# Audio tower on one core: MOE0's weights split in the first stage, logits by groups of four tiles, MOE1's rows scattered into the result

## The chip, the cores and the metric

The kernel runs on one core of a Trainium2 chip. The metric is the device time of one launch in microseconds (us). All work and all data movement of the launch is in it: inputs and the result lie in the device's DRAM.

## The reference

x is (4, 64, 750), taken as 4 batches of 750 tokens; the result is (4, 750, 192), 3000 tokens of E = 192. In f32:

```
h = token mixer(x)                       # three attention blocks over pooled rows, kernels of 3, 5, 7
h = h + linear_attention(layernorm(h))   # 12 heads, features [1, x/rrd, x*x/rd]
h = h + moe0(layernorm(h))               # rms norm, softmax of 8 logits, top 2,
                                         # silu(gate) * up, width 384, down, times the probability;
                                         # plus its own input
h = h + window_attention(layernorm(h))   # 12 heads of 64, relative positions
h = h + moe1(layernorm(h))               # softmax of 8 logits, top 1, gelu, width 768, biases,
                                         # times the largest probability
```

## The kernel before, in words

h is held in SBUF as 24 tiles of P = 125 tokens. Four stages follow each other, and between two of them `Stage.close` (L118 to L124) clears the semaphores on POOL, so nothing of one stage overlaps the next: `token_mixer_and_attention` (0 to 116 us), `moe` with MOE0 (121 to 413), `window_attention` (422 to 1588), `moe` with MOE1 (1592 to the end). Each engine has its own instruction list, written by hand in its block of the stage, and waits on semaphores; the order in a block is the order in which the engine works. SP issues the DMAs, POOL the indirect ones.

`moe` serves both expert stages. `w1` holds for each of eight experts four quarters: the first 128 rows rounded (quarter 0) and their remainder (1), and the last 64 rows rounded (2) and the remainder (3, of which the lower half is zeroed by POOL, L915). ACT rounds (`round_weights`, L1093 to L1095), DVE subtracts (`rest_of_weights`, L1181 and L1182), since products run as fp32r with the parts added up. The front of the stage: DVE makes statistics (L1149, L1153) and the reciprocals and squares around L1163, then normalises tile by tile (`n`, L1171; in MOE0 `xn` = n times the rms factor and the row of norm weights, L1175). PE transposes a tile in two halves of 96 columns (L986), ACT copies them (`xnT`, L1104), and PE multiplies (L977): the tile `xnT` is the stationary operand and the 8 columns of `wr` move. SP stores `xn` to X in DRAM (L850 to L854, eight DMAs). DVE copies the logits (L1198; MOE1 adds the bias row, L1200), ACT takes the exponential (L1109), DVE the softmax (L1204 to L1206), the best one or two experts (L1210 to L1219) and the mask (L1223 or L1225). PE ranks the tokens of each expert (L997, L998), and DVE derives positions (L1229 to L1250) and the expert of each slot tile (`eid`, L1237 to L1241). A slot tile is 128 tokens of one expert: 54 in MOE0, 31 in MOE1.

Token numbers are put into slots by products: `tile0` says which slot tile a token goes to (L1258), `lane1` which lane in it (L1263, one operation for each of `top`), `tile1` is tile0 times the token's number, in two parts: the tile number by POOL (L922), the row number by DVE (L1268). 48 products in MOE0, 24 in MOE1 (L1005), give `who`, from which DVE works out the row to write (`give`, L1280) and to read (`take`, L1286).

Then come the slot tiles, in a ring of four buffers (13 turns and 2 tiles in MOE0, 7 and 3 in MOE1). POOL gathers 128 rows of X into `xg` (L928) after copying their numbers (L939, L949); PE transposes them (L1012, L1013), ACT and DVE split them (L1112 to L1115, L1294 and L1295, `rest_of_tokens`), PE makes the first products (L1023), ACT applies Silu or Gelu (L1127, L1131), DVE multiplies (L1303), PE transposes the hidden rows (L1059), DVE copies (L1309), PE makes the second products (L1073), DVE copies `y` or adds the bias (L1321, L1325), and POOL scatters it to Y in DRAM (L933).

After MOE0, SP loads Y back into the room of the next stage; h += n was added on DVE ahead of the logits' copy (L1189). After MOE1, SP loads Y (L873, eight DMAs), DVE adds each tile times its probability to h (L1347, 24 operations), and SP stores h to the result (L882, eight DMAs).

In stage 1, ACT and DVE also round and split the attention's weights (`w4`, from `raw`), which SP stores as W4 for the third stage. In `window_attention`, a head has six chunks, and SP moves its row of maxima, transposed by PE, as a row of the stationary operand (`max_row`, L1614, six DMAs for a head on semaphore `s_md`); PE waits for them before the head's scores (L1971).

## Time and profile before

| | us |
|---|---|
| median of 3 runs | 1837.29 (1833.49 to 1843.19) |
| the profiled execution | 1845.31 |
| its span | 1843.6 |
| PE busy | 1575.8 (85%) |
| DVE busy | 1190.7 (65%) |
| ACT busy | 1000.7 (54%) |
| POOL busy | 350.5 (19%) |
| TensorE clock granted, mean | 0.895 |

The span runs from the first to the last instruction that the profiler saw; the launch adds 1.7 to it. Busy shares are means over stages of different kinds: the attention takes 63% of the span and keeps PE near full, while the low places among the page's forty slices, at 7 to 12%, 22% and 86 to 90% of the span and in its last slice, are fronts and ends of stages.

### The profile page before, as it was taken

The page shows a single profiled execution, that of the slowest core. Times are in us where ns is not written, and L with a number is a line of the kernel's source. Part 1 is how long each engine was busy: PE and PEld are TensorE (multiplying, and loading weights), DVE is VectorE, ACT ScalarE, POOL GpSimd, SP SyncE. Part 2 cuts the span into 40 slices and gives each one's busy share as a digit, 9 for nine tenths or more (in the row PEclk, how much of TensorE's full clock was granted, in tenths as well). Part 3 has the DMA queues.
Part 4 walks back from the last instruction along what each step waited for, and adds up shares of the span by engine and source line. Part 5 has one row for each costly group of instructions (what it writes and reads, how often), then busy time and mean ns, then how long its engine had stood idle before and what let it go on. Part 6 is the DMA issues. An engine that isn't in the chain of part 4 may idle for free. (4 is left out here: it accounts for less than half of the span.)

```text
span 1843.6 us, 32271 instructions
## 1 busy us (share of the span) xinstructions
PE 1575.8 (85%) x10779; PEld 1476.3 (80%) x10780; DVE 1190.7 (65%) x2207; ACT 1000.7 (54%) x1781; POOL 350.5 (19%) x495
## 2 busy tenths in 40 slices
PE   5864599983699999899899899899999899648993
PEld 4764588873599899899899899899899898538993
DVE  3588555546686786786687686687786686562333
ACT  4134133323578577678578678578578577233330
POOL 4040366652010010010010010010010010213441
PEclk6875699996899899999899999899999899658997
DMA  5034011118010010110010110010010100441114
GB/s 192 16 80 136 22 55 52 55 50 209 17 50 10 27 51 10 29 50 10 27 50 10 29 48 12 28 42 18 28 42 18 28 8 18 128 166 34 43 42 116
DMA packets 66847, 94.72 MB, mean 51 GB/s; under 512 B 17824, under 2 KB 52338, under 8 KB 66330
## 3 DMA queue, kind: packets, MB, share of 16 engines
q1 hardware_dynamic: 58026, 75.19, 14.0%
q0 software_dynamic: 8688, 17.80, 3.4%
q8 instruction: 78, 1.28, 0.3%
q14 instruction: 55, 0.45, 0.1%
HBM read 71.71 MB, written 21.06 MB: 50 GB/s over the span
## 5 line engine op out<-in xcount | busy, mean ns | idle before, releaser
L2471 DVE TENSOR_TENSOR a_Plo<-a_PT,a_Phi 125x756 fp32r<-125x756 f32 x288 | 281.8, 979 | 72.5 <-ACT a_PT L2196 71.4
L2196 ACT ACTIVATE a_Phi<-a_S 125x756 fp32r<-125x756 f32 x288 | 231.2, 803 | 156.8 <-PE a_O L1990 128.8
L2361 DVE TENSOR_REDUCE a_nmx<-a_M 125x1 f32<-125x752 f32 x248 | 232.7, 938 | 108.2 <-PE a_M L1865 107.1
L1685 POOL TENSOR_TENSOR a_qlo<-a_work,a_qhi 127x750 fp32r<-127x750 f32 x48 | 79.2, 1656 | 1019.3 <-PE a_S L1971 514.9
L2196 ACT ACTIVATE a_PT<-a_S 125x756 f32<-125x756 f32 x288 | 230.2, 799 | 0.0
L1023 PE MATMUL m_psG<-m_w,m_xT 128*128 x788 | 169.7, 355 | 5.4 <-DVE m_xT L1295 4.2
L1971 PE MATMUL a_S<-a_qhi,a_khi 128*125 128x378 f32 x576 | 154.0, 349 | 13.8 <-DMA a_qhi<-a_mrow 7.5
L1983 PE MATMUL a_O<-a_Phi,a_vhi 125*128 125x378 f32 x576 | 150.2, 342 | 1.4 <-issue 1.1
L1023 PEld LDWEIGHTS m_psG<-m_w,m_xT 128*128 128x128 f32 x788 | 138.7, 194 | 12.9 <-issue 11.5
L1971 PE MATMUL a_S<-a_qhi,a_klo 128*125 128x378 f32 x576 | 148.5, 339 | 0.0
L1971 PE MATMUL a_S<-a_qlo,a_khi 128*125 128x378 f32 x576 | 147.9, 338 | 0.0
L1990 PE MATMUL a_O<-a_Plo,a_vhi 125*128 125x378 f32 x576 | 147.6, 337 | 0.4 <-DVE a_Plo L2471 0.2
L1986 PE MATMUL a_O<-a_Phi,a_vlo 125*64 125x378 f32 x576 | 146.6, 336 | 0.0
L1073 PE MATMUL m_psY<-m_w,m_hidT 128*128 x696 | 128.0, 328 | 1.9 <-DVE m_hidT L1309 1.9
L1865 PE MATMUL a_M<-a_khi,a_qhi 127*125 127x376 f32 x496 | 128.7, 341 | 0.4 <-DVE a_nmx L2361 0.4
L1073 PEld LDWEIGHTS m_psY<-m_w,m_hidT 128*128 128x128 f32 x696 | 117.4, 191 | 2.4 <-issue 2.4
L1971 PEld LDWEIGHTS a_S<-a_qhi,a_khi 128*125 128x125 f32 x576 | 101.3, 190 | 19.2 <-DMA a_qhi<-a_mrow 6.8
L1990 PEld LDWEIGHTS a_O<-a_Plo,a_vhi 125*128 125x128 f32 x576 | 104.2, 189 | 14.0 <-DVE a_Plo L2471 3.7
L1112 ACT ACTIVATE m_xT<-m_psX 128x128 fp32r<-128x128 f32 x85 | 23.6, 277 | 168.8 <-PE m_psX L1013 149.1
L1983 PEld LDWEIGHTS a_O<-a_Phi,a_vhi 125*128 125x128 f32 x576 | 102.1, 190 | 10.7 <-issue 9.3
L933 POOL DMA_INDIRECT m_Y<-m_y,m_rows x85 | 84.0, 988 | 112.9 <-DVE m_y L1325 66.7
L1971 PEld LDWEIGHTS a_S<-a_qhi,a_klo 128*125 128x125 f32 x576 | 105.0, 189 | 0.0
(388 smaller groups left out, 3130.2 us busy)
## 6 DMA issues: line engine op xcount, KB each, us to landing
a_qhi<-a_rdens SPq DMA_DIRECT2D x48, 187.5 KB, 3.3
m_w<-in_m_w SPq DMA_DIRECT2D x16, 384.0 KB, 8.3
a_wkv<-a_w4k SPq DMA_DIRECT2D x8, 768.0 KB, 4.8
a_wq<-a_w4q SPq DMA_DIRECT2D x8, 768.0 KB, 6.3
a_wkv<-a_w4v SPq DMA_DIRECT2D x8, 768.0 KB, 5.9
a_qhi<-a_mrow SPq DMA_DIRECT2D x288, 0.5 KB
m_w<-in_m_w SPq DMA_DIRECT2D x8, 576.0 KB
m_X<-m_xn SPq DMA_DIRECT2D x8, 504.0 KB
```

The lines of the kernel that those rows point to most:

```text
L933: pool.indirect_dma_start(out=Y, out_offset=bass.IndirectOffsetOnAxis(ap=rows[:, j, 1:2], axis=0), in_=y[:, j, :], in_offset=None).then_in ...
L1023: last = nc.tensor.matmul(psG[buf][:, g, 0:half], tokens, w1[0:rows_, bass.ds(e, 1), k, g * half:(g + 1) * half].rearrange("d o f -> d (o ...
L1073: last = nc.tensor.matmul(psY[:, 0:E], hidT[:, k * 128:(k + 1) * 128], w2[:, bass.ds(here, 1), k, :].rearrange("f o e -> f (o e)"), start= ...
L1685: pool.tensor_tensor(qlo[0:ONE, u % HG % QLO, :], work[0:ONE, u % HG, 0:L], qhi[0:ONE, u % HG, :].bitcast(F32), ALU.subtract).then_inc(sg[ ...
L1865: last = nc.tensor.matmul(bank[0:P, a, 0:376], qhi[0:ONE, u % HG, c * P:(c + 1) * P], khi[0:ONE, u % HG, a * 374:a * 374 + 376], start=Tru ...
L1971: last = nc.tensor.matmul(psS[wd % 2][0:P, a, 0:HP], kk[:, u % HG, at], qq[:, PART[a]:PART[a] + HP], start=(x == 0), stop=(x == 2))
L1983: nc.tensor.matmul(psO[:, a, 0:HP], vhi[:, c, u % HG, :], Phi[:, wd % 2, at[a]], start=(c == 0), stop=False)
L1986: nc.tensor.matmul(psO[0:HD, a, 0:HP], vlo[:, c, u % HG, :], Phi[:, wd % 2, at[a]], start=False, stop=False)
L1990: last = nc.tensor.matmul(psO[:, a, 0:HP], vhi[:, c, u % HG, :], Plo[:, wd % 2, at[a]], start=False, stop=(c == CH - 1))
L2196: last = nc.scalar.activation(to[:, wd % 2, :].rearrange("p (a l) -> p a l", a=2), psS[wd % 2][0:P, :, 0:HP], ACT.Exp, scale=SCALE)
L2361: v.tensor_reduce(nmx[:, u % 2, c:c + 1], bank[0:P, :, 0:376], AX.XY, ALU.max, negate=True).then_inc(sg["max_ready"], 1)
L2471: v.tensor_tensor(Plo[:, wd % 2, :], PT[:, wd % 2, :], Phi[:, wd % 2, :].bitcast(F32), ALU.subtract).then_inc(sg["exp_rest"], 1)
```

## The change

**Stage 1.** SP also loads the router's weights, the norm row and MOE0's `w1`: experts 5 to 7 behind the attention's raw weights, 0 to 4 once W4 is stored. ACT rounds them between its other steps, DVE subtracts in the loop over batches, and POOL zeroes the lower halves, three quarters before it zeroes `w4`'s and five later. `w1` lies above everything else of the stage; `xc` and `sqd` share other tensors' room. The roundings of `w4` all stand ahead of the wait for the convolution.

**Logits.** The router's weights are padded to 32 columns. PE transposes four tiles (`turn_tiles`), then multiplies (`logits`): `wr` is stationary in one of four groups of 32 columns for each tile, and 125 columns of `xnT` move; ACT copies the 128 x 125 result, PE transposes it back (`logits_back`), and DVE copies all logits in two pieces. In MOE0 the `n` of even tiles is made by ACT; in MOE1 statistics and reciprocals are made batch by batch.

**From logits to rows.** The softmax's sum and reciprocal are made after `take`, on values that need them only then; so are h += n in MOE0 (four operations) and, in MOE1, five experts' subtractions. `eid` is made after the lanes. The second part of `tile1` is made by ACT in 24 scaled copies in MOE0, by DVE in MOE1, no longer by POOL. ACT applies Exp and then Silu or Gelu to one element ahead of time.

**MOE1's end.** X holds xn and h side by side, 384 wide, stored by 16 DMAs. Three bf16 parts of each token's probability are placed into slots by 24 more products (`probabilities`). For each slot tile DVE copies the gathered h row and forms y times probability plus h, and POOL scatters this into the result; rows of empty slots are left out by a bounds test. The load of Y, the 24 updates and the stores are gone.

**Attention.** `max_row` is one DMA.

```diff
+            def first_weights(e):
+                sp.dma_start(w1[:, e, 1, :].bitcast(F32), A["m0_w1"][0:128, e]).then_inc(s_w1[e], 16)
+                sp.dma_start(w1[0:64, e, 3, :].bitcast(F32), A["m0_w1"][128:E, e]).then_inc(s_w1[e], 16)
+            for e in range(BEHIND, NE):
+                first_weights(e)
...
             sp.wait_ge(s_w4, 48)
+            for e in range(BEHIND):
+                first_weights(e)
...
             pool.wait_ge(s_cst, 1)
+            for e in range(BEHIND, NE):
+                pool.memset(w1[64:128, e, 3, :].bitcast(F32), 0.0)
...
+            pool.wait_ge(s_diag, 1)
+            for e in range(BEHIND):
+                last = pool.memset(w1[64:128, e, 3, :].bitcast(F32), 0.0)
+            last.then_inc(s_cst, 1)
...
+            for e in range(BEHIND, NE):
+                round_weights(e)
+            round_weights(0)
...
+            for e in range(1, 4):
+                round_weights(e)
...
+                if b == 0:
+                    round_weights(4)
...
+                rest_of_weights(one, 0)
+                rest_of_weights(one, 1)
+                if two is not None:
+                    rest_of_weights(two, 0)
...
+            def store(tokens, b, to):
+                for ps in ROW_PARTS:
+                    sp.dma_start(X[b * L:(b + 1) * L, to:to + E].rearrange("(c p) e -> p c e", p=P)[ps],
+                                 tokens[ps, b * CH:(b + 1) * CH, :]).then_inc(s_X, 16)
+            if not cfg.gated:
+                for b in range(B):
+                    store(h, b, E)
             for b in range(B):
...
-                for b in range(B):
-                    for ps in ROW_PARTS:
-                        sp.dma_start(xn[ps, b * CH:(b + 1) * CH, :],
-                                     Y[b * L:(b + 1) * L, :].rearrange("(c p) e -> p c e", p=P)[ps]
-                                     ).then_inc(s_got[b], 16)
-                for b in range(B):
-                    sp.wait_ge(s_got[b], 16 * len(ROW_PARTS))
...
-                for b in range(B):
-                    sp.wait_ge(s_res, CH * (b + 1))
-                    for ps in ROW_PARTS:
-                        sp.dma_start(out[b].rearrange("(c p) e -> p c e", p=P)[ps],
-                                     h[ps, b * CH:(b + 1) * CH, :]).then_inc(s_out, 16)
-                sp.wait_ge(s_out, 16 * len(ROW_PARTS) * B)
...
-            pool.memset(w1[64:128, :, 3, :].bitcast(F32), 0.0).then_inc(s_z, 1)
-            pool.wait_ge(s_z, 3)
+            if not cfg.gated:
+                for e in range(NE):
+                    last = pool.memset(w1[64:128, e, 3, :].bitcast(F32), 0.0)
+                last.then_inc(s_z, 1)
+                pool.wait_ge(s_z, 3)
...
-            pool.wait_ge(s_num, 1)
-            pool.tensor_tensor(tile1[:, :, :, 1, :].rearrange("p k t s -> p (k t) s"),
-                               tile0[:].rearrange("p k t s -> p (k t) s"),
-                               num_t[:].rearrange("p k t -> p (k t)").unsqueeze(2).broadcast_to([P, top * NT, S]),
-                               ALU.mult).then_inc(s_who, 1)
...
+                if out is None:
+                    pool.indirect_dma_start(
+                        out=Y, out_offset=bass.IndirectOffsetOnAxis(ap=rows[:, j, 1:2], axis=0),
+                        in_=y[:, j, :], in_offset=None).then_inc(s_st[j], 16)
+                else:
+                    pool.indirect_dma_start(
+                        out=out.rearrange("b l e -> (b l) e"),
...
+            def logits(g):
+                pe.wait_ge(s_rc, GROUP * g + GROUP)
-                    last = nc.tensor.matmul(psX[0:P, 256 + NE * t:256 + NE * t + NE], xnT[:, t % RING, k, :],
+                    for z in range(GROUP):
+                        last = nc.tensor.matmul((psY, psX)[g % 2][32 * z:32 * z + 32, 0:P], wr[:, k, :],
+                                                xnT[:, GROUP * (g % 2) + z, k, :], start=(k == 0), stop=(k == 1))
+                last.then_inc(s_lt, 1)
...
+            def logits_back(g):
+                pe.wait_ge(s_lc, g + 1)
+                to = psH[0:P, 0, 128 * g:128 * g + 128] if g < 4 else psY[0:P, 128 * (g - 4):128 * (g - 4) + 128]
+                nc.tensor.transpose(to, lgT[:, g, :], ident[:]).then_inc(s_lg, 1)
...
+                turn_tiles(g)
+                if g >= 1:
+                    logits(g - 1)
+                if g >= 2:
+                    logits_back(g - 2)
...
-            pe.wait_ge(s_who, 2)
+            pe.wait_ge(s_who, 1)
             for k in range(top):
                 pe.wait_ge(s_b, k + 1)
                 for t in range(NT):
+                    if k == 0 and cfg.gated:
+                        pe.wait_ge(s_wt, t + 1)
...
+            def probabilities():
+                pe.wait_ge(s_part, 1)
+                for t in range(NT):
+                    last = nc.tensor.matmul(psY[:, 256:256 + PARTS * S], lane1[:, 0, t, :],
+                                            tileP[:, t, :, :].rearrange("p n s -> p (n s)"),
+                                            start=(t == 0), stop=(t == NT - 1))
+                last.then_inc(s_prob, 1)
...
+            def normalise(t):
+                nc.scalar.activation(n[:, t, :], h[:, t, :], ACT.Identity, bias=nmr[:, t:t + 1],
+                                     scale=rstd[:, t:t + 1]).then_inc(s_na, 1)
...
             act.wait_ge(s_ls, 1)
             nc.scalar.activation(lg[:], lg[:], ACT.Exp).then_inc(s_ex, 1)
+            nc.scalar.activation(warm[:], ident[0:1, 0:1], ACT.Silu if cfg.gated else ACT.Gelu)
+            if not cfg.gated:
+                for e in range(soon, NE):
+                    round_weights(e)
+            if cfg.gated:
+                act.wait_ge(s_num, 1)
+                for t in range(NT):
+                    nc.scalar.activation(tile1[:, :, t, 1, :], tile0[:, :, t, :], ACT.Copy, scale=float(t)
...
-            link(v.tensor_reduce(lm[:], lg[:], AX.X, ALU.add))
-            link(v.reciprocal(lm[:], lm[:]))
-            link(v.tensor_tensor(pr[:], lg[:], lm[:].unsqueeze(2).broadcast_to([P, NT, NE]), ALU.mult))
+            pr = lg
...
-            link(v.tensor_tensor(ecmp[:], iots[:].unsqueeze(2).broadcast_to([1, S + 2, NE]),
-                                 cum[0:1, :].unsqueeze(1).broadcast_to([1, S + 2, NE]), ALU.is_ge))
-            link(v.tensor_reduce(eidf[:], ecmp[:], AX.X, ALU.add))
-            link(v.tensor_scalar(eidf[:], eidf[:], float(NE - 1), None, ALU.min))
-            v.tensor_copy(eid[:], eidf[:]).then_inc(s_eid, 1)
             link(v.tensor_tensor(cnt[:], cum[:], nt_[:], ALU.subtract))
...
-            dve.wait_ge(s_X, 16 * len(ROW_PARTS) * B)
+            dve.wait_ge(s_num, 1)
+            for k in range(top):
+                last = v.tensor_scalar(tile1[:, k, :, 0, :], tile0[:, k], (num_p, num_2)[k][:], None, ALU.mult)
+            if cfg.gated:
+                last.then_inc(s_who, 1)
+            else:
+                v.tensor_tensor(tile1[:, 0, :, 1, :], tile0[:, 0], num_t[:].unsqueeze(2).broadcast_to([P, NT, S]),
+                                ALU.mult).then_inc(s_who, 1)
+            dve.wait_ge(s_X, stored)
             for k in range(top):
                 v.tensor_tensor(lane1[:, k], iotl[:].unsqueeze(1).broadcast_to([P, NT, SLOT]),
                                 lane[:, k, :].unsqueeze(2).broadcast_to([P, NT, SLOT]), ALU.is_equal
                                 ).then_inc(s_b, 1)
-            dve.wait_ge(s_num, 1)
-            v.tensor_scalar(tile1[:, :, :, 0, :].rearrange("p k t s -> p (k t) s"),
-                            tile0[:].rearrange("p k t s -> p (k t) s"), num_p[:], None, ALU.mult).then_inc(s_who, 1)
-            for e in range(soon, NE):
-                rest_of_weights(e)
+            link(v.tensor_tensor(ecmp[:], iots[:].unsqueeze(2).broadcast_to([1, S + 2, NE]),
+                                 cum[0:1, :].unsqueeze(1).broadcast_to([1, S + 2, NE]), ALU.is_ge))
+            link(v.tensor_reduce(eidf[:], ecmp[:], AX.X, ALU.add))
+            link(v.tensor_scalar(eidf[:], eidf[:], float(NE - 1), None, ALU.min))
+            v.tensor_copy(eid[:], eidf[:]).then_inc(s_eid, 1)
...
+            if not cfg.gated:
+                for e in range(3, NE):
+                    rest_of_weights(e)
+            link(v.tensor_reduce(lm[:], lg[:], AX.X, ALU.add))
+            link(v.reciprocal(lm[:], lm[:]))
+            for k in range(top):
+                link(v.tensor_tensor(pe_[:, k, :], pe_[:, k, :], lm[:], ALU.mult))
+            if cfg.gated:
+                for b in range(B):
+                    at_ = slice(b * CH, (b + 1) * CH)
+                    v.tensor_tensor(h[:, at_, :], h[:, at_, :], n[:, at_, :], ALU.add)
+            if not cfg.gated:
+                for x in range(PARTS):
+                    link(v.tensor_copy(part[:, x, :], pe_[:, 0, :] if x == 0 else lm[:]))
+                    if x + 1 < PARTS:
+                        link(v.tensor_tensor(lm[:], pe_[:, 0, :] if x == 0 else lm[:], part[:, x, :], ALU.subtract))
+                dve.wait_ge(s_w, 16 * (NE + 3))
+                v.tensor_tensor(tileP[:], tile0[:, 0].unsqueeze(2).broadcast_to([P, NT, PARTS, S]),
+                                part[:].rearrange("p x t -> p t x").unsqueeze(3).broadcast_to([P, NT, PARTS, S]),
+                                ALU.mult).then_inc(s_part, 1)
...
+                if not cfg.gated:
+                    v.tensor_copy(hres[:, j % RING, :], xg[:, j % RING, E:2 * E]).then_inc(s_hr, 1)
...
-                            "p o e -> p (o e)"), ALU.add).then_inc(s_y, 1)
+                            "p o e -> p (o e)"), ALU.add).then_inc(s_b2, 1)
+                        dve.wait_ge(s_b2, RING * i + (j + 1))
+                        dve.wait_ge(s_hr, RING * i + (j + 1))
+                        v.scalar_tensor_tensor(y[:, j, :], y[:, j, :], prob[:, bass.ds(RING * i + j, 1)],
+                                               hres[:, j, :], ALU.mult, ALU.add).then_inc(s_y, 1)
...
-                        for c in range(CH):
-                            sp.dma_start(qhi[ONE:ONE + 1, u % HG, c * P:(c + 1) * P].bitcast(F32),
-                                         mrow[c:c + 1, u % 2, :].bitcast(F32)).then_inc(s_md[u % 2], 16)
+                        sp.dma_start(qhi[ONE:ONE + 1, u % HG, :].bitcast(F32),
+                                     mrow[:, u % 2, :].bitcast(F32)).then_inc(s_md[u % 2], 16)
```

How the order of instructions moves, at three places. First PE at the start of MOE0 (psG takes transposed tiles, psX, psY and psH logits). Before, the last tiles and the ranks:

```order
L977 MATMUL m_psX<-m_wr,m_xnT 125x8 x2
L986 MATMUL m_psG<-ident,m_xn 96x125 x2
L977 MATMUL m_psX<-m_wr,m_xnT 125x8 x6
L997 MATMUL m_psG<-m_msk,m_tri 125x192
L998 MATMUL m_psG<-m_msk,m_ones 128x192
```

and now the last two groups:

```order
L1086 MATMUL m_psH<-ident,m_lgT 125x128
L1068 MATMUL m_psG<-ident,m_xn 96x125 x8
L1079 MATMUL m_psY<-m_xnT,m_wr 32x125 x8
L1086 MATMUL m_psH<-ident,m_lgT 125x128
L1079 MATMUL m_psX<-m_xnT,m_wr 32x125 x8
L1086 MATMUL m_psY<-ident,m_lgT 125x128 x2
L1101 MATMUL m_psG<-m_msk,m_tri 125x192
```

The pairs of one tile became eights of four tiles, with a transpose back behind each group.

Second DVE in MOE0 from `take` to the first slot tile. Before:

```order
L1286 CAST m_take<-m_who 128x54
L1294 TENSOR_TENSOR m_xT<-m_psX,m_xT 128x128
L1295 TENSOR_TENSOR m_xT<-m_psX,m_xT 64x128
L1303 TENSOR_TENSOR m_hid<-m_act_g,m_psG 128x384
L1309 COPY m_hidT<-m_psH 128x384
```

and now:

```order
L1476 CAST m_take<-m_who 128x54
L1481 TENSOR_REDUCE m_lm<-m_lg 125x24
L1482 RECIPROCAL m_lm<-m_lm 125x24
L1484 TENSOR_TENSOR share<-share,m_lm 125x24 x2
L1488 TENSOR_TENSOR h<-h,m_n 125x1152 x4
L1506 TENSOR_TENSOR m_xT<-m_psX,m_xT 128x128
L1507 TENSOR_TENSOR m_xT<-m_psX,m_xT 64x128
```

Eight operations came between `take` and the first subtraction of tokens.

Third ACT in MOE0 from the exponential into the loop (m_lg are the logits, m_act_g the gate's half). Before:

```order
L1109 ACT_TABLE_LOAD
L1109 ACTIVATE m_lg<-m_lg 125x192
L1112 ACTIVATE m_xT<-m_psX 128x128
L1115 ACTIVATE m_xT<-m_psX 64x128
L1138 UNCONDITIONAL_BRANCH
L1138 ISA
L1126 ISA
L1127 ACT_TABLE_LOAD
L1127 ACTIVATE m_act_g<-m_psG 128x384
```

and now:

```order
L1260 ACTIVATE m_lg<-m_lg 125x192
L1261 ACT_TABLE_LOAD
L1261 ACTIVATE m_warm<-ident 1x1
L1268 ACTIVATE m_tile<-m_tile 125x2x54 x24
L1272 ACTIVATE m_xT<-m_psX 128x128
L1275 ACTIVATE m_xT<-m_psX 64x128
L1298 UNCONDITIONAL_BRANCH
L1298 ISA
L1286 ISA
L1287 ACTIVATE m_act_g<-m_psG 128x384
```

The table load that stood behind the loop's first branch, and was met in every turn, stands ahead of the loop.

## Rows read from the trace of the kernel before

**Rows 1.** Stretches: us, busy (x) of PE, PEld, DVE, ACT, POOL, PEclk, DMA, GB/s
```profile
134.00:138.00 4.00, 4.00 (x22) 3.78 (x22) 4.00 (x14) 3.92 (x8) 0.00 (x0) 0.50 1.02 290
...
1564.00:1565.00 1.00, 1.00 (x34) 1.00 (x32) 0.00 (x0) 0.20 (x1) 0.00 (x0) 1.00 0.09 18
```

**Rows 2.** Timeline of the end: start us, us, engine, line, operation
```profile
1817.26 0.96 POOL L933 DMA_INDIRECT m_Y<-m_y,m_rows  x1 [3.10 <-DVE m_y L1325]
...
1819.75 5.68 SPq L873 DMA_DIRECT2D m_xn<-m_Y  x8
```

**Rows 3.** Timeline of MOE0's front, to the copy of the logits
```profile
123.59 5.21 POOL L915 MEMSET m_w<- 64x6144 f32 x1
...
124.14 4.69 DVE L1163 TENSOR_SCALAR m_msq<-m_msq 125x24 f32<-125x24 f32 x1
...
132.99 0.63 PE L986 MATMUL m_psG<-ident,m_xn 125*96 125x125 f32 x2
...
133.41 0.85 PE L977 MATMUL m_psX<-m_wr,m_xnT 96*125 96x8 f32 x4
...
153.10 4.95 DVE L1189 TENSOR_TENSOR h<-h,m_n 125x4608 f32<-125x4608 f32 x1
...
159.19 0.36 DVE L1198 COPY m_lg<-m_psX 125x192 f32<-125x192 f32 x1 [1.14 <-issue]
```

**Rows 4.** Timeline of PE in the attention: products in two column halves
```profile
1564.58 1.85 PE L1815 MATMUL a_S<-a_work,a_rv 96*64 96x81 f32 x48
```

**Rows 5.** Timeline of MOE0, expert ids to `take`, DVE, POOL and PE
```profile
171.69 0.61 DVE L1237 TENSOR_TENSOR m_ecmp<-m_iots,m_cum 1x448 f32<-1x448 f32 x1
...
177.62 2.86 DVE L1258 TENSOR_TENSOR m_tile<-m_at,m_iott 125x2592 bf16<-125x2592 bf16 x1
...
180.39 3.35 DVE L1263 TENSOR_TENSOR m_lane<-m_iotl,m_lane 125x3072 bf16<-125x3072 bf16 x1
...
180.56 7.56 POOL L922 TENSOR_TENSOR m_tile<-m_tile,m_num_t 125x2592 bf16<-125x2592 bf16 x1 [48.99 <-DVE m_tile L1258]
...
191.26 0.88 DVE L1268 TENSOR_SCALAR m_tile<-m_tile,m_num_p 125x2592 bf16<-125x2592 bf16 x1
...
192.20 4.50 PE L1005 MATMUL m_psY<-m_tile,m_lane 125*128 125x108 bf16 x48 [23.12 <-DVE m_tile L1268]
...
199.88 0.19 DVE L1286 CAST m_take<-m_who 128x54 uint32<-128x54 f32 x1
```

**Rows 6.** Timeline of MOE0, first expert tile
```profile
205.33 0.29 DVE L1294 TENSOR_TENSOR m_xT<-m_psX,m_xT 128x128 fp32r<-128x128 f32 x1 [5.26 <-ACT m_xT L1115]
...
208.82 3.56 PE L1023 MATMUL m_psG<-m_w,m_xT 128*128 x10 [2.10 <-DVE m_xT L1295]
```

**Rows 7.** MOE0's loop: line 1127's table loads, two gathers of POOL
```profile
L1127 ACT ACT_TABLE_LOAD  x13: 1283/1283/1283, 210.9 to 388.6; - x13
...
284.31 0.99 POOL L928 DMA_INDIRECT m_xg<-m_X,m_rows  x1 [0.79 <-issue]
...
287.69 0.98 POOL L928 DMA_INDIRECT m_xg<-m_X,m_rows  x1 [0.79 <-issue]
```

**Rows 8.** Line 1614 (row of maxima): who waited for it, us, times
```profile
  PE a_S L1971: 7.5, 6
```

**Rows 9.** MOE1: stores to X, weights, logits, first products, waits for line 1131
```profile
1603.15 13.29 SPq L853 DMA_DIRECT2D m_X<-m_xn  x8
...
L1095 ACT ACTIVATE m_w<-m_w 64x768 fp32r<-64x768 f32 x8 | 6.7, 843 | 0.1
...
L1181 DVE TENSOR_TENSOR m_w<-m_w 128x768 fp32r<-128x768 f32 x8 | 7.6, 954 | 9.4 <-ACT m_w L1095 9.4
...
1632.93 0.34 DVE L1200 TENSOR_TENSOR m_lg<-m_psX,m_row 125x192 f32<-125x192 f32 x1
...
1664.91 1.64 PE L1023 MATMUL m_psG<-m_w,m_xT 128*128 x4 [2.09 <-DVE m_xT L1295]
...
  PE m_psH L1059: 3.0, 7
```

402 lines of the change are left out of this document (253 added, 149 removed).

## The prediction

> **What bounds the kernel now.** I first read the busy shares: TensorE works 85% of the span, so time can only be won where it idles or runs badly. Then the time by stage, read from the timeline: the idle stretches lie in the two router fronts (the logits to the first expert tile) and after the last tile, not in the long window attention. Then the stretches with the granted clock: in MOE0's logits PE is 4.00 of 4 us busy, but at 0.50 of its clock, the 1.2 GHz level, although it is busy throughout; late in the attention it runs at 1.00 [rows 1]. Last the timeline of the end, of both fronts and of POOL in the loop. The reader should see in them: a store, a load back and an update in series at the end [rows 2]; a 5.21 us POOL memset beside a DVE operation that takes 4.69 us [rows 3]; DVE comparisons of whole tables ahead of the first product [rows 5]; an activation table load in every turn [rows 7].
>
> **The change, part by part** (us, against the profiled execution).
>
> *The end: -23.2.* The last scatter is issued at 1817.26 for 0.96; SP goes on at 1819.75 [rows 2]. All that follows (eight loads of Y, 24 updates, eight stores) lasts to the span's end, 1843.6, and goes. What stays is the scatter's own landing, 1819.75 and some 0.6 of ending: 1820.4. Bounds: a scatter into the result with its bounds test may land up to 3 later.
>
> *Stage 1: +1.0.* Added are 18 DMAs, 24 roundings on ACT, 16 subtractions on DVE and eight memsets on POOL. ACT and DVE idle there between dependent steps, and the roundings (0.84 each) are put into those gaps; the loads are issued behind the raw weights. Three memsets stand ahead of the one that DVE's first operations run beside; rows 3 show what that can cost: an operation of 24 columns held for 4.69. From 0 (all in gaps) to +3 (one such hold, part of it on the path); I take +1.0, nearer the covered end, since only one small operation is exposed.
>
> *MOE0, before the logits: -4.4.* The memset is gone from this stage, and with it the hold: 4.69 less the 0.3 of a free one [rows 3].
>
> *MOE0, logits: -10.6.* Before: the hold ends at 128.83, the copy of the logits starts at 159.19, so 30.4 for 24 tiles. The two transposes of a tile take 0.42 (133.41 less 132.99), that is 0.21 for 125 moving columns. Now four tiles form a group: 8 transposes, 1.7; 8 products of two records with 125 moving columns in four column groups; one transpose back, 0.2. The products would be 16 x 0.21 = 3.4 in series and 0.8 if four run side by side. Two column halves do run side by side in the attention: 48 records of 81 columns in 1.85 [rows 4], 38.5 ns each, where 81 columns at the transposes' pace, at double clock, are 68. So a group costs 2.7 to 3.8; six are 16 to 23. ACT has its copies and half the normalising, about 14, below that. I take the lower end, as the groups write different columns like the halves of rows 4, plus the 3.4 at start and end that the 30.4 holds today: 19.8.
>
> *MOE0, logits to `take`: -9.1.* Off the path go three softmax operations (0.35 each, -1.1; one of this size is the 0.34 of rows 9) and the expert ids (two operations of 0.61 and two small ones, -1.6 [rows 5]). Today tile0 ends at 180.48, the two lane comparisons last from 180.39 to 191.26 beside POOL's 7.56 (the first alone 3.35), tile1 0.88, the 48 products 4.50, ending 196.70, and `who` starts some 0.5 later, as DVE still works on weights; `take` is at 199.88 [rows 5]. After: tile1 about 1.0, two lanes of 3.3 with POOL silent, the first 24 products under the second lane, 2.3 for the last: 190.5. That is -6.2, and -0.5 for the weights. The two operations more in `who` are +0.45, the split copy +0.2, Exp with its table loaded -0.4. ACT's 24 scaled copies lie under the lanes; at 0.25 each they would just fit, and if they do not, up to +3.
>
> *MOE0, `take` to the first products: +0.9.* DVE now does the reduction, reciprocal, two multiplications (1.1) and h += n (4.95 [rows 3]) before `rest_of_tokens`: 6.1 where it idled 5.26 waiting for the gathered rows [rows 6]. PE waits for that operation (208.82).
>
> *MOE0's loop: -13.9.* 13 table loads of 1283 ns, from 210.9 to 388.6 [rows 7]: 12 intervals, 14.81 each turn. The order shows none in the new loop. POOL gathers one tile in 3.38 (284.31 to 287.69), four in 13.52, a floor under any turn. 13 x 1.283 = 16.7 would be the whole; down to POOL's floor it is 12 x 1.29 = 15.5. I take 1.07 a turn, as the first turn is slow for other reasons. Bounds -8 (half is absorbed by waits) and -19. The Trainium skill, ScalarE: Activation LUTs, What ACT_TABLE_LOAD costs, adds a drain of about 1380 ns to each switch; by it, as an estimate, the loop would lose 13 x 2.66 = 34.6. No row separates such a drain.
>
> *Window attention: -6.* PE waited 7.5 in all, six times, for the row of maxima [rows 8]. Six issues for a head become one, so that its row lands sooner by five issues of SP; each of the waits is 1.25 long in the mean, and I take most of it. Bounds 0 and -7.5.
>
> *MOE1, front: -6.1.* ACT loses 15 of 24 weight roundings before the logits, 15 x 0.843 = 12.6; batchwise statistics let it begin some 4 sooner (estimate: a quarter of the statistics instead of all), less the added copies and Exp's table, about 2.6: -14. Off the chain go the softmax operations and the ids, -2.2. DVE then does after `take` ten subtractions (9.5), the denominator and five small parts (1.9) and tileP (2232 elements; tile0's 2592 took 2.86, so 2.5), 13.9 in all against a wait of about 5.3: +8.6. And 16 stores to X instead of 8, which took 13.29 [rows 9]: their landing may come after DVE wants it; 0 to +5, taken +1.5. Together from -11 to +2.
>
> *MOE1, loop and first tile: -1.7.* PE waited 3.0 over seven table loads [rows 9]; DVE's two added operations per tile give back 1.0; the probabilities' products add 0.3 to the first tile.
>
> **Sum:** +1.0 -4.4 -10.6 -9.1 +0.9 -13.9 -6 -6.1 -1.7 -23.2 = -73.1. The profiled execution took 1845.3, 8.0 above the median of the runs: 1772 for it, and 1764 against the median of 1837.3.
>
> **The rivals.**
> (a) *Column groups run in series.* For: today's PE is saturated at half clock, and groups alternate between transposes and products; against: rows 4. A group is then 5.3, six 31.8: MOE0's logits end 15 later than forecast, MOE1's 12: 1791. The Trainium skill, TensorEngine Tiling (Array Packing), Key Properties, says that a switch of tiling mode drains TensorE, which speaks against the change; it also says that tiles work in parallel, and with that rows 4 agree.
> (b) *MOE0's loop keeps its length:* POOL's gather chain or DVE sets the turn already and the table load was under it. For: the 3.38 floor is close to the mean of 3.70; against: the turn without the load fits 13.52 to 0.01. Then +13.9: 1778.
> (c) *The clock rises in the fronts,* since their PE work is denser. Against: at 4.00 of 4 busy it did not [rows 1]. Placement products (4.50) and transposes would halve: -8, 1756.
> (d) *Slower:* MOE1's loop becomes bound by POOL's indirect DMAs, as gathered rows are twice as long and the scatter tests bounds. One mechanism, 31 tiles, today 152.4 from 1664.91 to 1817.26, 4.91 each. To lose the 73 and 9 more, a tile must take 7.6; POOL's 3.38 holds two indirect DMAs of 0.98 and 1.4 of other work, so each would have to cost 3.1, over three times its row. Then 1846 and more.
>
> **How the numbers follow.** Forecast 0.67, (b) 0.15, (a) 0.08, (c) 0.07, (d) 0.03. The time is the forecast's. Its own unknowns (MOE0's loop 5, MOE1's front 6, logits 6, stage 1 2, the end 3) partly cancel: about 15 either way. Upwards the range takes in (b) and reaches almost to (a), 1790; downwards (c) with a faster loop, 1744. 0.5% is 9.2 us, about what a measurement can tell from no change. All cases but (d) lie far below; a mix of mishaps that just reaches it is 0.01: faster 0.97, same 0.01, slower 0.02.
>
> **What would show it.** Right: the last scatter followed by the end within 3; the logits' copy about 144 to 146 with transposes of four tiles 1.7 apart and products under 2; no table load between 200 and 400 and turns near 13.6; `take` to the first products near 10; PE's wait for the maxima's row near 1.5. Wrong: products of a group taking 3.4 (a), turns still above 14.5 (b), a front at clock 1.00 (c), tiles of MOE1 above 5 with PE waiting for gathered rows (d), or DVE waiting for X's stores before the lanes in MOE1.

## The result, and the profile after

The changed kernel takes 1778.53 us (median of 4 runs, 1776.25 to 1782.84) where the kernel before takes 1839.24 (4 runs): 60.7 us less, a ratio of 0.967 with a 95% interval from 0.9648 to 0.9692. In a second comparison on one chip it took 1777.42 (5 runs) against 1837.06 (9 runs), 59.6 less, ratio 0.9675. The profiled execution took 1779.27 with a span of 1777.5, so it is near its median, while the profiled execution before stood 6 above its own.

| stretch, us | before | after | difference | forecast |
|---|---|---|---|---|
| start to MOE0's first statistics | 121.2 | 122.0 | +0.8 | +1.0 |
| MOE0: to the copy of the logits | 38.0 | 20.7 | -17.3 | -15.0 |
| MOE0: logits to `take` | 40.7 | 31.5 | -9.2 | -9.1 |
| MOE0: `take` to the first products | 8.9 | 9.9 | +0.9 | +0.9 |
| MOE0: first products to the last scatter | 204.5 | 193.5 | -11.1 | -13.9 |
| change of stage | 8.8 | 8.3 | -0.5 | 0 |
| window attention | 1170.1 | 1161.7 | -8.3 | -6 |
| MOE1: to the copy of the logits | 40.7 | 29.5 | -11.2 | -14 |
| MOE1: logits to `take` | 23.3 | 21.1 | -2.2 | -0.7 |
| MOE1: `take` to the first products | 8.7 | 16.7 | +8.0 | +8.6 |
| MOE1: first products to the last scatter | 152.3 | 154.5 | +2.2 | -1.7 |
| last scatter to the end | 26.3 | 8.3 | -18.0 | -23.2 |
| span | 1843.6 | 1777.5 | -66.1 | -73.1 |

(The forecast of -0.7 for MOE1's chain is -2.2 and the +1.5 for X's stores.) The busy shares of the page, which answer to those in the table before the prediction:

```profile
PE 1545.6 (87%) x10815; PEld 1432.0 (81%) x10816; DVE 1198.3 (67%) x2259; ACT 990.7 (56%) x1818; POOL 343.4 (19%) x507
```

The stretches in MOE0's front; the columns are those of [rows 1]:

```profile
130.00:134.00 4.00, 4.00 (x28) 2.50 (x28) 3.40 (x11) 3.59 (x12) 0.00 (x0) 0.50 0.68 189
...
134.00:138.00 4.00, 4.00 (x49) 3.08 (x48) 3.04 (x10) 3.31 (x12) 0.00 (x0) 0.77 0.40 117
...
138.00:142.00 4.00, 3.92 (x63) 2.60 (x61) 1.87 (x6) 3.28 (x13) 0.00 (x0) 1.00 0.74 204
```

TensorE is busy all through, as before, but its granted clock rises from 0.50 to 1.00, the 2.4 GHz level, at 135.8 (0.77 is the mean of the stretch in which it rises), and falls back at 146.1, behind the front. Before, it was 0.50 from 119 to 218, though the stretch of [rows 1] was as busy, 4.00 of 4 us. The timeline of that front (start, duration, engine, line):

```profile
125.20 0.23 DVE L1329 TENSOR_SCALAR m_msq<-m_msq 125x24 f32<-125x24 f32 x1
...
131.19 1.06 PE L1079 MATMUL m_psY<-m_xnT,m_wr 96*32 96x125 f32 x16
...
132.18 1.90 PE L1068 MATMUL m_psG<-ident,m_xn 125*96 125x125 f32 x8
...
140.36 0.64 PE L1079 MATMUL m_psY<-m_xnT,m_wr 96*32 96x125 f32 x16
...
142.67 0.29 DVE L1382 COPY m_lg<-m_psH 125x128 f32<-125x128 f32 x1 [2.72 <-PE m_psY L1086]
```

The operation that the memset held for 4.69 [rows 3] takes 0.23 in its place (125.20). A group's products, 16 records of 125 columns, take 1.06 at half clock, where one after the other, at the transposes' pace of 0.21, they would take 3.4; they start four at a time, and each four 0.21 behind the last. Eight transposes take 1.9. At full clock the products are 0.64. The logits' copy comes at 142.67 instead of 159.19.

From `tile0` to the first products, the rows that answer to [rows 5, 6]:

```profile
161.05 4.49 ACT L1268 ACTIVATE m_tile<-m_tile 125x108 bf16<-125x108 bf16 x24 [15.13 <-DVE m_tile L1438]
...
161.99 6.62 DVE L1451 TENSOR_TENSOR m_lane<-m_iotl,m_lane 125x3072 bf16<-125x3072 bf16 x2
...
168.67 2.34 PE L1111 MATMUL m_psY<-m_tile,m_lane 125*128 125x108 bf16 x24 [0.91 <-DVE m_lane L1451]
...
174.16 0.19 DVE L1476 CAST m_take<-m_who 128x54 uint32<-128x54 f32 x1
...
175.45 5.17 DVE L1488 TENSOR_TENSOR h<-h,m_n 125x1152 f32<-125x1152 f32 x4
...
180.54 0.28 DVE L1506 TENSOR_TENSOR m_xT<-m_psX,m_xT 128x128 fp32r<-128x128 f32 x1
...
184.03 3.37 PE L1129 MATMUL m_psG<-m_w,m_xT 128*128 x10 [2.10 <-issue]
```

The two parts of tile1 that DVE makes take about 0.5 each, the two lane comparisons 6.62 together without POOL beside them, ACT's 24 copies 4.49 under them, and half of the products lies under the second lane. h += n takes 5.17 between `take` and the first split of tokens (180.54), which the gathered rows no longer hold.

MOE0's loop: the gate's activations (source line 1287) have no table load among them any more, and the stretch of the loop reads, in the columns of [rows 1],

```profile
L1287 ACT ACTIVATE m_act_g<-m_psG x54: 490/491/493, 186.1 to 371.3; 128x384 f32<-128x384 f32 x54
...
200.00:370.00 170.00, 168.18 (x1022) 158.15 (x1020) 94.30 (x243) 44.79 (x145) 111.21 (x196) 1.00 0.19 57
```

54 activations start from 186.1 to 371.3, so 13.98 for a turn of four tiles; before they started from 212.2 to 407.1, 14.71 a turn. TensorE is now busy for 168.18 of 170 us. Its clock also rises sooner after the first products: at 187.0, 3.0 us behind them, where before it rose at 218.0, 9.2 us behind them.

MOE1, the front, its chain and the first tile:

```profile
1550.21 6.05 POOL L998 MEMSET m_w<- 64x768 f32 x8
...
1551.63 4.74 DVE L1314 TENSOR_SCALAR m_xn<-h,m_mv,m_rstd 125x192 f32<-125x192 f32 x6
...
1558.68 1.83 DVE L1314 TENSOR_SCALAR m_xn<-h,m_mv,m_rstd 125x192 f32<-125x192 f32 x6
...
1576.95 0.29 DVE L1384 TENSOR_TENSOR m_lg<-m_psH,m_row 125x128 f32<-125x128 f32 x1 [1.01 <-PE m_psY L1086]
...
1598.02 0.18 DVE L1476 CAST m_take<-m_who 128x31 uint32<-128x31 f32 x1
...
1605.93 0.94 DVE L1310 TENSOR_TENSOR m_w<-m_w 64x768 fp32r<-64x768 f32 x1
...
1607.09 0.45 PE L1118 MATMUL m_psX<-ident,m_xg 128*128 128x128 f32 x1 [11.10 <-issue]
...
1608.80 2.48 DVE L1496 TENSOR_TENSOR m_tileP<-m_tile,m_part 125x2232 bf16<-125x2232 bf16 x1
...
1611.20 0.28 DVE L1506 TENSOR_TENSOR m_xT<-m_psX,m_xT 128x128 fp32r<-128x128 f32 x1
...
1614.67 1.64 PE L1129 MATMUL m_psG<-m_w,m_xT 128*128 x4 [2.08 <-DVE m_xT L1507]
```

Three things stand out. The first six normalising operations take 4.74 while POOL's memsets run, the next six 1.83. The transposes of the first slot tile start at 1607.09, right behind the last subtraction of weights (1605.93 and 0.94), although `take` was ready at 1598.02: TensorE waits for all weights ahead of its transposes. And tileP (2.48) stands between them and the first split of tokens (1611.20).

One tile of MOE1's loop:

```profile
1664.05 0.36 DVE L1539 TENSOR_TENSOR m_y<-m_psY,m_b 128x192 f32<-128x192 f32 x1 [2.27 <-PE m_psY L1190]
...
1664.53 0.42 DVE L1543 SCALAR_TENSOR_TENSOR m_y<-m_y,m_prob,m_hres 128x192 f32<-128x192 f32 x1
...
1664.86 0.95 DVE L1523 COPY m_hidT<-m_psH 128x768 f32<-128x768 f32 x1
...
1665.96 2.21 PE L1190 MATMUL m_psY<-m_w,m_hidT 128*128 x12
...
1668.75 0.36 DVE L1539 TENSOR_TENSOR m_y<-m_psY,m_b 128x192 f32<-128x192 f32 x1 [2.15 <-issue]
```

DVE adds the bias (L1539), makes y times probability plus h (L1543), and only then copies the transposed hidden rows (hidT, L1523, to 1665.81), for which the second products (1665.96) wait; from y to y it is 4.70. And the end:

```profile
1769.19 0.97 POOL L1017 DMA_INDIRECT out<-m_y,m_rows  x1 [3.54 <-DVE m_y L1543]
```

No work follows this scatter, yet the span ends only at 1777.5. What stands between is the scatter's landing and then POOL's DRAIN at the end of the stage's block. Its rows after and before (min/median/max in ns of the two in the trace, the one behind MOE0 and the one behind MOE1, and when each starts):

```profile
L786 POOLq DRAIN  x2: 802/3171/5540, 380.2 to 1771.7; - x2
...
L718 POOLq DRAIN  x2: 802/3170/5537, 416.1 to 1820.0; - x2
```

After the change, POOL's and SP's waits for the last scatter end 2.1 behind its issue (1771.3), the DRAIN runs from 1771.7 for 5.54, and the span ends 0.2 behind it. Before, a DRAIN as long ran from 1820.0 to 1825.6, under the load of Y and the updates.

### The profile page after: what moved, and what is told of

Read it like the earlier page. It is cut to its first block and busy times, and to the rows that moved or that the text cites. A ratio compares the mean times of both kernels' runs of the same rounds, so it can differ in the third digit from the quotient of the medians.

```text
span 1777.5 us, 32284 instructions
## 1 busy us (share of the span) xinstructions
PE 1545.6 (87%) x10815; PEld 1432.0 (81%) x10816; DVE 1198.3 (67%) x2259; ACT 990.7 (56%) x1818; POOL 343.4 (19%) x507
## 3 DMA queue, kind: packets, MB, share of 16 engines
q1 hardware_dynamic: 52606, 72.92, 13.9%
## 5 line engine op out<-in xcount | busy, mean ns | idle before, releaser
L2209 PEld LDWEIGHTS a_O<-a_Plo,a_vhi 125*128 125x128 f32 x576 | 104.1, 189 | 13.9 <-DVE a_Plo L2690 3.7
L2202 PEld LDWEIGHTS a_O<-a_Phi,a_vhi 125*128 125x128 f32 x576 | 102.1, 190 | 10.7 <-issue 9.3
L2190 PEld LDWEIGHTS a_S<-a_qlo,a_khi 128*125 128x125 f32 x576 | 104.0, 187 | 0.0
```

What stands on the lines that cost most here:

```text
L2190: last = nc.tensor.matmul(psS[wd % 2][0:P, a, 0:HP], kk[:, u % HG, at], qq[:, PART[a]:PART[a] + HP], start=(x == 0), stop=(x == 2))
L2202: nc.tensor.matmul(psO[:, a, 0:HP], vhi[:, c, u % HG, :], Phi[:, wd % 2, at[a]], start=(c == 0), stop=False)
L2209: last = nc.tensor.matmul(psO[:, a, 0:HP], vhi[:, c, u % HG, :], Plo[:, wd % 2, at[a]], start=False, stop=(c == CH - 1))
```

## The experiments

Each kernel's stretches are read between the same marks as in the table, in one profiled execution of each. Each experiment but the last two was run once. The chains from the logits to `take` and from `take` to the first products repeat within 0.1 where no edit touches them; the others spread: stage 1 (120.6 to 122.7), MOE0's logits (19.2 to 20.8; in the three of 19.2 and 19.3 TensorE's clock rose 9.2 us after the stage's start, in the others 13.5 to 14.3), MOE0's loop (191.0 to 194.1), MOE1's front (29.3 to 30.2) and MOE1's loop (153.9 to 154.5). The attention is told of below.

**Table loads in the loops.** In the changed kernel:

```diff
-            nc.scalar.activation(warm[:], ident[0:1, 0:1], ACT.Silu if cfg.gated else ACT.Gelu)
```

> The changed kernel without the activation of Silu or Gelu on one element ahead of the loops, so that each turn loads its table again. Theory (table loads were on the turn's path, as forecast): MOE0's stretch from the first expert products to the last scatter, 193.5 us in the changed kernel, grows by 10 to 14, MOE1's (154.5) by 2 to 4. Rival (TensorE sets the turn in the changed kernel anyway and another part of the change shortened the loop): both grow by under 3.

Its source line 1286, the gate's activations, which start from 186.8 to 380.4:

```profile
L1286 ACT ACT_TABLE_LOAD  x13: 1283/1283/1283, 185.5 to 361.7; - x13
```

MOE0's stretch was 203.2 (+9.7 against the changed kernel's profiled execution), MOE1's 156.3 (+1.8). Against the other three executions on the same chip (192.5 to 193.7 for MOE0, and 153.9 and 154.0 for MOE1 where that loop has no edit) it is 9.5 to 10.7 and 2.4. So the table loads make most of the -11.1, and a load costs some 0.75, not its 1.283: the rest is hidden, and there is no sign of more than its own duration. The 1.3 that is left between 203.2 and the 204.5 of before is less than the first turn alone lost (14.43 against 16.42), in which the clock rose 6 us sooner; that the clock is the cause was not tested. The expectation gave 10 to 14 and 2 to 4; the measured growths lie at or near its lower bounds.

What sets a turn without the loads shows in the control of the last section, the same kernel in another execution:

```profile
288.19 0.99 POOL L1006 DMA_INDIRECT m_xg<-m_X,m_rows  x1 [0.79 <-POOL m_rows L1037]
...
291.58 0.99 POOL L1006 DMA_INDIRECT m_xg<-m_X,m_rows  x1 [0.80 <-POOL m_rows L1037]
```

There 43 of the last 50 gathers follow each other at POOL's own pace, 3.38 to 3.42, with `y` ready before POOL comes to scatter it; a turn is 13.78 and the stretch 191.0. In the profiled execution of the table above 30 of 50 do, and for the others POOL waits for `y`; a turn is 13.98 and the stretch 193.5. Behind the first five, no gather of this loop follows at less than 3.37 in any execution. So POOL's 3.38 is a floor that the new loop touches, and TensorE is nearly full as well, busy for 168.18 of 170 us here and 163.29 of 165 (200 to 365) in the control. What decides between 191 and 194 no run tells; the three executions near 191 ran on one chip, the other experiments on two others.

**DVE's order in MOE1's loop.**

```diff
                         dve.wait_ge(s_b2, RING * i + (j + 1))
                         dve.wait_ge(s_hr, RING * i + (j + 1))
                         v.scalar_tensor_tensor(y[:, j, :], ...
-                    if j < ahead:
-                        hidden_columns(i, j + 1)
```

with the two removed lines put ahead of these three.

> In MOE1's loop DVE copies the transposed hidden rows (hidT) before its second operation on y, not after. Theory (DVE's added operation stands ahead of the copy for which the second products wait, and lengthens a tile from 4.6 to 4.7 us): the tile's pitch falls by 0.1 or more, the stretch from the first expert products to the last scatter from 154.5 to 150 to 152. Rival (TensorE's own work sets the pitch): unchanged within 0.7.

```profile
1653.34 0.96 DVE L1523 COPY m_hidT<-m_psH 128x768 f32<-128x768 f32 x1
...
1654.21 0.41 DVE L1546 SCALAR_TENSOR_TENSOR m_y<-m_y,m_prob,m_hres 128x192 f32<-128x192 f32 x1
...
1654.88 2.20 PE L1190 MATMUL m_psY<-m_w,m_hidT 128*128 x12
```

The hidT copy is done at 1654.30, 0.6 before the second products, and no longer holds them. The stretch took 152.7, 1.8 less (1.3 less than in the executions of 153.9 and 154.0), short of the 2.5 to 4.5 that was expected. The tile's pitch stayed at 4.67 in the mean, above the 4.58 between the starts of second products before (1684.04 to 1688.62), and the twelve products take 2.20 where they took 2.11 before.

The traces show where this comes from, though no run removed it. TensorE's block waits for `s_y` ahead of the second products, since DVE must have read psY before it is written again. Before, the operation that reads psY raised `s_y`; now the second operation on y does, which reads no PSUM. In this run that operation ends at 1654.62 and the products start at 1654.88, and in all of the loop's other tiles they start 0.25 to 0.28 behind it. The first product is then on time, but the second starts 0.25 behind it instead of the 0.17 of before. The table-load run shows the other case: where a load held TensorE and both operations had ended 0.47 or more ahead of the products, these take 2.11 again, and in the next tile, where hidT ended 0.14 ahead, 2.21:

```profile
1647.52 0.96 DVE L1522 COPY m_hidT<-m_psH 128x768 f32<-128x768 f32 x1
...
1648.95 2.11 PE L1190 MATMUL m_psY<-m_w,m_hidT 128*128 x12
...
1653.67 2.21 PE L1190 MATMUL m_psY<-m_w,m_hidT 128*128 x12
```

The pitch is longer by some 0.09 in each of 30 tiles, which makes 2.7. A wait for `s_b2`, the first operation's semaphore, would be enough for psY; it was not tried.

**MOE1's memsets later.**

```diff
+                pool.wait_ge(s_n, NT)
                 for e in range(NE):
                     last = pool.memset(w1[64:128, e, 3, :].bitcast(F32), 0.0)
```

> MOE1's eight memsets on POOL wait until DVE has normalised all tiles. Theory (the memsets held DVE's first normalising operations, 4.74 us for six instead of 1.83, and so the logits): the copy of the logits comes 2 to 4 us earlier after the stage's start (29.5 us in the changed kernel). Rival (ACT's roundings and copies set the logits' end): earlier by under 1.

```profile
1548.06 1.83 DVE L1315 TENSOR_SCALAR m_xn<-h,m_mv,m_rstd 125x192 f32<-125x192 f32 x6
...
1571.03 0.29 DVE L1385 TENSOR_TENSOR m_lg<-m_psH,m_row 125x128 f32<-125x128 f32 x1 [1.01 <-PE m_psY L1087]
```

The first six operations took 1.83, and the logits' copy came 27.1 after the stage's start, 2.4 earlier. That is what the theory asked for. It also accounts for most of what the forecast of -14 missed here.

**The end, I.** The last three slot tiles go to Y, without the bounds test:

```diff
                 pool.wait_ge(s_y, RING * turns + j + 2)
-                scatter(j)
+                pool.indirect_dma_start(
+                    out=Y, out_offset=bass.IndirectOffsetOnAxis(ap=rows[:, j, 1:2], axis=0),
+                    in_=y[:, j, :], in_offset=None).then_inc(s_st[j], 16)
```

> The last three slot tiles of MOE1 are scattered to the internal tensor Y without the bounds test; their rows are missing from the result. Theory (landing in the result with the bounds test takes some 4 us longer than in Y): from the last scatter's issue to the end 4 to 5 us instead of 8.3. Rival (the end of a launch behind an indirect DMA costs this whatever its target): 8 to 8.6.

```profile
1766.05 0.96 POOL L1051 DMA_INDIRECT m_Y<-m_y,m_rows  x1 [3.57 <-DVE m_y L1545]
```

The span ended at 1774.6, 8.5 behind this issue. The target and the bounds test cost nothing here, and the rival holds: POOL's DRAIN takes 5.54 in this run too.

**The end, II.** Neither POOL nor SP handles the last three slot tiles; SP waits for DVE:

```diff
-                scatter(j)
...
+            if not cfg.gated:
+                sp.wait_ge(s_y, S + 1)
```

> The last three slot tiles of MOE1 are computed but not scattered; SP waits for DVE's last operation on y instead. The last indirect DMA is then issued some 9 us before that operation. Theory (the end waits for POOL's indirect DMAs to be wound up, about 8 us after the last one is issued): the span ends 1 to 3 us after DVE's last operation. Rival (a launch ends some 6 us after its last work, whatever it is): the span ends 6 us or more after it.

```profile
1756.05 1.02 POOL L1019 DMA_INDIRECT out<-m_y,m_rows  x1 [1.57 <-DVE m_y L1546]
...
1768.32 0.42 DVE L1546 SCALAR_TENSOR_TENSOR m_y<-m_y,m_prob,m_hres 128x192 f32<-128x192 f32 x1
```

The last indirect DMA is issued at 1756.05, DVE's last operation ends at 1768.74, and the span at 1769.2, 0.5 later, even sooner than the 1 to 3 of the theory. The DRAIN's row says why:

```profile
L786 POOLq DRAIN  x2: 802/3048/5295, 380.6 to 1758.5; - x2
```

It takes 5.30 here and starts at 1758.5, so it is over at 1763.8, under the last tiles. So a launch can end right behind its last operation. What costs 8.3 when the scatter is last is its landing and the waits for it, some 2.5, and then this DRAIN, which stands last in POOL's list. Why it takes 5.5 behind MOE1 in both kernels and 0.80 behind MOE0, which also ends with indirect DMAs, no run shows.

**The row of maxima.** The changed kernel with the six DMAs of before.

> The changed kernel with six DMAs for a head's row of maxima, as before the change. Theory (the single DMA is worth what TensorE waited, up to 7.5 us): waits of TensorE for a_mrow come back with about 7 us, and the attention stage takes 1166 to 1172 us instead of the 1156 to 1162 of five runs of the changed stage. Rival (that difference comes from elsewhere, such as the state in which the stage starts): the stage stays within 1156 to 1163.

Who waited for them (source line 1834):

```profile
  PE a_S L2191: 7.5, 6
```

The waits of [rows 8] are back to the digit, 7.5 over six times, and with the one DMA there are none at all. The stage took 1165.4, between what the theory and the rival gave; ten executions with one DMA took 1156.2 to 1164.6, 1159.8 in the mean. So the stage's time alone does not prove it, but the difference to the mean, 5.6, agrees with the waits. The 1170.1 of the profiled execution before is longer than both. The medians differ by 60.7 and the spans by 66.1, so some 5 us of the latter are that execution's own, and they probably lie here.

**The order of a group's products.**

```diff
-                for k in range(2):
-                    for z in range(GROUP):
+                for z in range(GROUP):
+                    for k in range(2):
```

> The eight products of a group of four tiles in another order: both halves of a tile (same column group) one after the other, instead of four column groups in turn. Theory (column groups work side by side only when neighbours in the instruction stream address different groups): 16 records take 1.7 us or more at half clock instead of 1.06, and MOE0's stretch to the logits' copy (20.7 us) grows by 1 to 4. Rival (their overlap does not depend on the order, or the records are bound by loading weights): unchanged within 0.3 us each.

In this run every product of every stage, also of those ahead of the edit, took about 1.6 times as long, and the kernel 3006.51; it says nothing of the edit. Where this trace has records of the granted clock, from 2903 on, they read 0.56 up to 2991, a value that no other run has. It was run again.

> The kernel of e7_tile_by_tile once more, since in that run TensorE took 1.6 times as long for every product of all stages, also ahead of the edited place. Theory (column groups work side by side only when neighbours in the instruction stream address different groups): 16 records take 1.7 us or more at half clock instead of 1.06, and MOE0's stretch to the logits' copy (20.7 us) grows by 1 to 4. Rival (the order does not matter): unchanged within 0.3 us each. If the slowness of all stages comes again, it belongs to this kernel and not to the chip's state in that run.

```profile
131.27 1.08 PE L1079 MATMUL m_psY<-m_xnT,m_wr 96*32 96x125 f32 x16
```

The 16 records take 1.08 and 0.66 instead of 1.06 and 0.64, the logits' copy comes after the same 20.7, and the slowness is gone. The order does not matter: four records of one column group in a row run as well beside the other groups' as four that alternate. The 1.06 is little more than one group's four records in series, 4 x 0.21 = 0.84.

**MOE1's first tokens ahead.** `rest_of_tokens` for the first two slot tiles goes ahead of the softmax's sum, the parts and tileP, and in TensorE's block

```diff
-            if not cfg.gated:
-                pe.wait_ge(s_wl, NE)
-                pe.wait_ge(s_z, 3)
             for j in range(2):
                 pe.wait_ge(s_in[j], 16)
...
             pe.wait_ge(s_xc, 2)
+            if not cfg.gated:
+                pe.wait_ge(s_wl, NE)
+                pe.wait_ge(s_z, 3)
```

> In MOE1 DVE splits the first two slot tiles (rest_of_tokens) right after the weights, ahead of the probabilities' parts and tileP, and TensorE waits for the weights only after it has transposed the first two slot tiles. Theory (tileP and TensorE's early wait stand between take and the first products): that stretch falls from 16.7 to 10.5 to 12.5 us, with up to 1 given back in the loop's stretch. Rival (the gathered rows are late themselves): falls by under 2.

```profile
1595.05 0.18 DVE L1476 CAST m_take<-m_who 128x31 uint32<-128x31 f32 x1
...
1600.02 0.45 PE L1118 MATMUL m_psX<-ident,m_xg 128*128 128x128 f32 x1 [7.01 <-DMA m_xg<-m_X,m_take]
...
1607.38 1.64 PE L1129 MATMUL m_psG<-m_w,m_xT 128*128 x4 [2.17 <-DVE m_xT L1485]
...
1611.21 1.96 PE L1138 MATMUL m_psY<-m_tileP,m_lane 125*128 125x93 bf16 x24 [0.27 <-DVE m_tileP L1508]
```

TensorE transposes at 1600.02 under DVE's subtractions, and from `take` to the first products it is 12.3, 4.3 less. The probabilities' products waited 0.27 for tileP. The loop's stretch stayed at 154.5.

**Together.** These three edits, and in MOE0 half of h += n moved ahead of DVE's wait for the logits.

> The changed kernel with four edits together: MOE1's memsets after the normalising, rest_of_tokens ahead of the probabilities, the hidT copy ahead of DVE's second operation on y, and in MOE0 half of h += n moved into DVE's wait for the logits. Theory (each works on its own stretch): -2.4, -4.4, -1.8 and -0.9, together 9 to 10 us less than the changed kernel, about 1769. Rival (they share a cover and give back, in the loop above all): less than 5.

> The changed kernel as it is, on the same chip as e9_together, as a control: 1776 to 1783 us.

```profile
139.50 2.62 DVE L1380 TENSOR_TENSOR h<-h,m_n 125x1152 f32<-125x1152 f32 x2
...
142.31 0.29 DVE L1387 COPY m_lg<-m_psH 125x128 f32<-125x128 f32 x1 [0.18 <-PE m_psY L1087]
...
179.14 0.29 DVE L1489 TENSOR_TENSOR m_xT<-m_psX,m_xT 128x128 fp32r<-128x128 f32 x1 [1.43 <-ACT m_xT L1276]
```

Two of the four operations (2.62) fill the gap in front of the logits' copy, and DVE waits for the gathered rows again at 179.14; `take` to the first products is 8.9. The kernel takes 1769.13 (5 runs, ratio to before 0.9629, interval 0.9615 to 0.9643), the changed kernel on the same chip 1777.42 (0.9675, 0.9661 to 0.969). The intervals are apart: 8.3 us, of the 9 to 10 expected, and the stretches show each edit at its place: 27.1, 12.3, 152.9 and 8.9. It beats both kernels.

## Why the prediction was right

The forecast was 1764, the measured time 1778.53, inside the range of 1744 to 1790, and faster, as 0.97 of the chances had it. 60 of the 73 us came.

*What held as it was worked out.* The operation that MOE0's memset held takes 0.23 without it. The chain from the logits to `take` came out at -9.2 for -9.1, term by term: the softmax and the ids gone, the lanes at 3.3 each without POOL, the first products under the second lane, ACT's copies under the lanes. h += n stands in place of the wait for rows (+0.9 for +0.9), and DVE's added work after `take` in MOE1 is +8.0 for +8.6. These are sums of durations that stood in the trace, along one engine's order. Stage 1 came out at +0.8 for +1.0, but that says little: the same stage spreads by 2.1 between executions.

*MOE0's logits: -13.1 for -10.6.* The groups do run side by side, as the low end of the range had it, and part of case (c) came with it: the clock rose within the front. That part is luck. With it, three eights of transposes took 1.25, 1.31 and 1.09 instead of 1.90 and four groups of products 0.64 instead of 1.06, up to 3.7 together; without it the term might have fallen short of 10.6 by about one. The -8 of (c) did not come, since the clock was back at 0.50 for all that follows up to the loop. The text spoke against (c) with the row at 4.00 of 4 busy; being busy did not tell the two fronts apart.

*MOE0's loop: -11.1 for -13.9.* The mechanism was right, and so was the floor under a turn, "POOL gathers one tile in 3.38": the new loop reaches that pace for 30 of 50 gathers here and for 43 of 50 in the control. What was too large is the term's size: 1.07 a turn was taken, and the run with the loads back gives 0.75. What keeps a turn above four times 3.38, 13.52, is, as far as the traces show, that TensorE was nearly full too: in the loop before it was busy for 162.18 of 170 us (230 to 400), 95%, and is now for 168.18 of 170; the text did not ask what TensorE's own work leaves. How much of the 2.8 is that and how much the execution is open: the control's 191.0 would be -13.6 against the same 204.5. As an estimate, the figure of the Trainium skill, ScalarE: Activation LUTs, What ACT_TABLE_LOAD costs, with its drain of 1380 ns, would have given 34.6; here a load of 1283 ns was worth 0.75, since TensorE had other work under it, and nothing shows a drain beyond it.

*Window attention.* The -6 was the right size: 7.5 of waits are gone, and the stage is 5.6 shorter in the mean. The -8.3 of the table holds chance.

*MOE1's front: -11.2 for -14 and no wait for X.* The term left out a cost that the same text had priced for MOE0: the memsets stay in MOE1 and now meet the normalising operations, which were brought forward. It is 2.4. The wait for X's stores, put at 1.5, did not come: the lanes start at once behind tile1.

*MOE1's loop: +2.2 for -1.7.* The loads were worth 1.8 to 2.4, where 3.0 was taken. The step that failed is "DVE's two added operations per tile give back 1.0". They cost some 4: 1.3 to 1.8 by the place of the second operation on y, ahead of hidT. The rest, some 2.5, stays when hidT goes first, since the second products then wait for `s_y`, which the change moved from the operation that reads psY to the one behind it; that this wait is the cause is read from the traces and was not tested by taking it out.

*The end: -18.0 for -23.2.* The step that failed is "What stays is the scatter's own landing, 1819.75 and some 0.6 of ending". Behind the landing stands POOL's DRAIN of 5.54, so that the end takes 8.3 from the scatter's issue and not 3.1. Its row could be read in the trace before, from 1820.0 to 1825.6, where it lay under the load back.

*The shortfall.* The spans fell by 66.1 for 73.1. The end missed 5.2, MOE1's loop 3.9, MOE0's loop 2.8 and MOE1's front 2.8; MOE0's logits (2.3), the attention (2.3), the wait for X's stores (1.5) and tenths elsewhere gave 7.6 back. The other half of the 14.5 by which the median missed is the last line of the sum, 1772 less 8.0: it took the profiled execution's surplus over its median for the same after the change. The changed kernel's profiled execution stood only 0.7 above its median.

*The rivals.* (a) fell: in series a group's products would have taken 3.4, they took 1.06. The Trainium skill, TensorEngine Tiling (Array Packing), Key Properties, has tiles work in parallel, and the trace agrees; of the drain at a switch of mode the trace shows at most what lies between the last product and the next transpose, and no gap there exceeds a few tenths. (b) fell: the loop lost 11.1, and 9.7 of it comes back with the loads. (c) came in part, as told above. (d) fell: a gather of rows twice as long and a scatter with the bounds test take POOL 0.99 and 1.02, as before.

## What to carry to other kernels

Two engines can stand at the floor of a loop together; a turn then stays above both floors, and taking the stall away gives less than the room above the lower one. Ask how far the same stretch moves between executions of one kernel before a miss of its size is put down to a step: here it was 3 us. When work is brought forward, ask again which operations now meet it: a memset that was harmless in one place can hold another engine's first operations. And an operation put on an engine inside a loop is cheap by its duration only if it stands behind the one that the bound engine waits for, and if the semaphore that frees a buffer stays with the operation that reads the buffer. Last, when work at the end of a launch is taken out, look at what each engine still did under it, its sequencer's DRAIN too.
